# Gate and up from bare FP4 values in three of four scale groups, the PSUM bank rescaled three times per tile, and weight pieces spread from the second to last chunk on

## The reference, cut to what matters

```python
s_full = jnp.repeat(s, group_size, axis=1)
return vals * s_full
...
w_gu = _dequant_fp4(gate_up_packed, gate_up_scales, GROUP_SIZE)
w_down = _dequant_fp4(down_packed, down_scales, GROUP_SIZE)
gate_up = jnp.einsum('bsh,oh->bso', x, w_gu)
gate, up = (gate_up[..., :I], gate_up[..., I:])
h = jax.nn.silu(gate) * up
y = jnp.einsum('bsi,hi->bsh', h, w_down)
rms = jnp.sqrt(jnp.mean(y * y, axis=-1, keepdims=True) + EPS)
return y / rms
...
x = _layernorm(x + _L0_attn_ref(x, L0_attn_Wq, L0_attn_Wk, L0_attn_Wv, L0_attn_Wo, L0_attn_rms_w), axis=-1)
x = _layernorm(x + _L0_xattn_ref(x, fside_BxS2xS2_0, ctx_1024), axis=-1)
x = _layernorm(x + _L0_ffn_ref(x, L0_ffn_gate_up_packed, L0_ffn_gate_up_scales, L0_ffn_down_packed, L0_ffn_down_scales), axis=-1)
```

## Time and profile before

| | us |
|---|---|
| median of 3 runs (772.44 to 775.64) | 773.85 |
| profiled execution | 770.9 |
| its span | 769.1 |
| TensorE busy | 706.7 (92%) |
| VectorE busy | 495.7 (64%) |
| ScalarE busy | 379.9 (49%) |
| GpSimd busy | 195.7 (25%) |
| attention to the last piece | 0 to 345.8 |
| FFN | 345.8 to 769.1 |

### The profile page before, as it was taken

The page is one execution under the profiler, slowest core; times in us unless marked ns, Lnnn a source line. Parts: engine busy times, 40 slices in busy tenths (PEclk is TensorE's granted clock), DMA queues, the critical chain, the costliest instruction groups (busy, mean ns, idle before and its releaser), DMA issues.

```text
span 769.1 us, 11695 instructions
## 1 busy us (share of the span) xinstructions
PE 706.7 (92%) x4565; PEld 569.7 (74%) x4574; DVE 495.7 (64%) x956; ACT 379.9 (49%) x613; POOL 195.7 (25%) x229
## 2 busy tenths in 40 slices
PE   5899998999999899649999999999989999999993
PEld 4688787877777787536787867878767878778882
DVE  4658668784576855776856586858668666743334
ACT  5244463355634372384473655635473736552334
POOL 0544444343644366841021100102000211000000
PEclk9899999999999999769999999999999999999998
DMA  9500200100320040021002120000430001200031
GB/s 335 195 20 1 56 2 3 54 2 28 107 73 2 28 152 1 1 109 55 1 7 77 55 73 37 2 28 0 164 110 0 1 29 57 108 1 1 0 110 55
DMA packets 25408, 41.17 MB, mean 54 GB/s; under 512 B 5002, under 2 KB 7690, under 8 KB 25226
## 3 DMA queue, kind: packets, MB, share of 16 engines
q1 hardware_dynamic: 23194, 37.40, 14.1%
q10 hardware_dynamic: 2160, 3.02, 1.1%
HBM read 28.88 MB, written 11.53 MB: 53 GB/s over the span
## 4 chain that ended last, share of the span: by engine, by line
PE 66%; DVE 19%; ACT 8%; DMA 2%; issue 2%; POOL 1%; ACTq 0%; DVEq 0%; POOLq 0%
PE ps L1726 20%; PE ps L1742 13%; PE ps L1309 10%; DVE act_s L383 4%; PE ps L1393 3%; PE ps L1348 3%; PE ps L534 2%; PE ps L1703 2%; PE ps L543 2%; PE ps L1704 2%; DMA rms_col<-in_L_attn_rms_w_dram 2%; DVE masked L1228 2%; PE ps L1376 2%; PE ps L1369 1%; PE ps L1357 1%
## 5 line engine op out<-in xcount | busy, mean ns | idle before, releaser
L1726 PE MATMUL ps<-x2T_hi,weights 128*128 128x512 f32 x528 | 163.3, 390 | 0.0
L1726 PEld LDWEIGHTS ps<-x2T_hi,weights 128*128 128x128 f32 x528 | 99.2, 188 | 19.9
L1742 PE MATMUL ps<-weights,h_hi 128*128 128x512 f32 x352 | 110.3, 394 | 3.2 <-DVE h_lo L1588 3.2
L1726 PE MATMUL ps<-x2T_lo,weights 128*128 128x512 f32 x264 | 106.8, 405 | 0.3 <-DVE ps L1593 0.3
L1611 DVE TENSOR_TENSOR silu<-ps,silu 128x512 f32<-128x512 f32 x44 | 30.3, 689 | 99.3 <-PE ps L1726 99.1
L1309 PE MATMUL ps<-wqkv_lo,xT_hi 128*128 128x512 f32 x192 | 81.0, 422 | 9.0 <-DVE wqkv_lo L1177 5.0
L1742 PEld LDWEIGHTS ps<-weights,h_hi 128*128 128x128 f32 x352 | 65.4, 188 | 17.6 <-DVE h_lo L1588 3.9
L1309 PE MATMUL ps<-wqkv_hi,xT_lo 128*128 128x512 f32 x192 | 76.3, 397 | 0.0
L1309 PE MATMUL ps<-wqkv_hi,xT_hi 128*128 128x512 f32 x192 | 76.3, 397 | 0.0
L1105 POOL TENSOR_TENSOR rot<-qkv,tab 128x256 f32<-128x256 f32 x64 | 44.6, 731 | 114.6 <-ACT qkv L994 114.6
L1506 ACT ACTIVATE silu<-ps 128x512 f32<-128x512 f32 x44 | 26.3, 598 | 86.4 <-PE ps L1726 86.4
(11 more groups left out here) (190 smaller groups left out, 1535.2 us busy)
## 6 DMA issues: line engine op xcount, KB each, us to landing
w<-in_fside_BxS2xS_dram SPq DMA_DIRECT2D x4, 1024.0 KB, 7.7
x_dram<-xb SPq DMA_DIRECT2D x4, 1024.0 KB, 4.3
xc<-x_dram SPq DMA_DIRECT2D x4, 1024.0 KB, 5.5
x_in<-in_x_dram SPq DMA_DIRECT2D x15, 256.0 KB, 3.4
xb<-x_dram SPq DMA_DIRECT2D x3, 1024.0 KB, 5.5
out_dram<-xc SPq DMA_DIRECT2D x3, 1024.0 KB, 4.3
z<-in_x_dram SPq DMA_DIRECT2D x3, 768.0 KB, 4.6
x_dram<-z SPq DMA_DIRECT2D x3, 768.0 KB, 3.5
```

The lines of the kernel that those rows point to most:

```text
L1726: last = nc.tensor.matmul(dst[:, :], lhs, rhs, start=False, stop=(k == NK - 1 and n == 2), skip_group_check=True)
L1742: last = nc.tensor.matmul(ps[c][:, :], lhs, rhs, start=(it == 0 and n == 0), stop=(it == NI - 1 and n == 2))
```

## The change

Groups 0 to 2 of gate and up are now bare (`BARE = 3`). After group 0 the bank is multiplied by s0/s1, after group 1 by s1/s2, after group 2 by s2; then group 3 follows scaled. So a half has 2+2+2+3 matmuls. The ratios are made once, on VectorE behind chunk 1 (`column_ratios`). Each bare pair but the first waits for the rescale before it. Bare pieces need no diagonal and no low part; every second of them is now copied by VectorE. The pieces start in chunk 14 and are spread differently: 13 in chunks 14 and 15, 9 behind chunk 15, 13 in FFN batch 0. The norm of the last attention batch (z) moves behind them into batch 0. Expert and output steps have new places, and place 1.5 now exists on all engines.

```diff
-EXPERT_STEPS = {"w_maxima": 2, ..., "round_x": 10, "clip_x": 10, "scale_w": 11, ...
+EXPERT_STEPS = {"w_maxima": 0, ..., "round_x": 10.5, "clip_x": 10, "scale_w": 10.5, ...
-OUTPUT_STEPS = {"rms": 2, "residual": 3, "moments": 14, "root": 21, "output": 26}
+OUTPUT_STEPS = {"rms": 1.5, "residual": 3, "moments": 15, "root": 21, "output": 27}
-UNSCALED = 0
+BARE = 3
-FIRST_BESIDE = 27
-PIECES_AT = {(14, "end"): (0, 1, 2), (15, "masks"): (3, 4, 5), (15, "split"): (6, 7),
-             (15, "end"): tuple(range(8, FIRST_BESIDE))}
+FIRST_BESIDE = 22
+PIECES_AT = {(14, "masks"): (0,), (14, "split"): (1, 2), (14, "end"): (3, 4, 5), (15, "masks"): (6, 7, 8, 9), (15,
+    "split"): (10, 11, 12), (15, "end"): (13, 14, 15, 16, 17, 18, 19, 20, 21)}
-PIECE_STEPS = {0: 27, 1: 28, 2: 29, 3: 30, 4: 31, 5: 32, 11: 33, 20: 34}
+PIECE_SLOTS = (0, 1.5, 2, 2, 3, 3, 5, 5, 7, 11, 11, 20, 27)
+LATE_STEPS = {"z_moments": 1, "z_root": 1.5, "z_shift": 2, "z_x1": 4.5}
...
     def lo(self, dve, m):
+        elif self.copied_by[m] == "dve":
+            dve.wait_ge(full, at + 1)
+            self.nc.vector.tensor_scalar(self.parts(m)[0], bank[:, 0:self.count(m) * P], 1.0, None, ALU.mult)\
+                .then_inc(drained, 1)
...
+        def column_ratios():
+            nc.vector.tensor_scalar(ratios, scales, 0.0, TINY, ALU.is_equal, ALU.mult).then_inc(ratio_step, 1)
+            nc.vector.tensor_tensor(ratios, scales, ratios, ALU.add).then_inc(ratio_step, 1)
+            nc.vector.reciprocal(inverse[:, first], ratios[:, later]).then_inc(ratio_step, 1)
+            nc.vector.tensor_tensor(ratios[:, first], scales[:, first], inverse[:, first], ALU.mult)\
+                .then_inc(weights.gate_up_cols_set, 1)
...
         def inner_tile(b, it, beside):
             hidden_hi(b, it)
             beside(3 * it + 1)
-            if it + 1 < NI:
-                scale_up(b, it + 1)
+            for k in range(BARE):
+                if it + 1 < NI:
+                    scale_up(b, it + 1, k)
+                if k == 0:
+                    beside(3 * it + 1.5)
             beside(3 * it + 2)
...
         def inner_tile(b, it, beside):
             if it + 1 < NI:
-                scale_gate(b, it + 1)
+                scale_gate(b, it + 1, 0)
             hidden_lo(b, it)
+            beside(3 * it + 1.5)
+            for k in range(1, BARE):
+                if it + 1 < NI:
+                    scale_gate(b, it + 1, k)
             beside(3 * it + 2)
...
+        def bare(b, it, k, half):
+            dst, scaled, part = ((ps[4], gate_scaled, gate_part), (ps[5], up_scaled, up_part))[half]
...
+            if k > 0:
+                pe.wait_ge(scaled, (b * NI + it) * BARE + k)
+            elif it > 0:
+                pe.wait_ge(h_done if half else silu_done, b * NI + it)
+            [values] = weights.gate_up(k, half, it)
+            nc.tensor.matmul(dst[:, :], values, x2T_lo[:, k, :], start=(k == 0), stop=False, skip_group_check=True)
+            nc.tensor.matmul(dst[:, :], values, x2T_hi[:, k, :], start=False, stop=True, skip_group_check=True)\
+                .then_inc(part, 1)
...
-            for k in range(1, NK):
+            for k in range(BARE, NK):
...
-            def next_unscaled(c):
+            def next_bare(c):
+                if it + 1 < NI:
+                    if c > 0:
+                        bare(b, it + 1, c - 1, 1)
+                    if 0 < c < BARE:
+                        bare(b, it + 1, c, 0)
                 if c == 1:
-                    if it + 1 < NI:
-                        unscaled_up(b, it + 1)
                     beside(3 * it + 1.5)
```

More of the change, by code:

```diff
@@ L154, in weight_pieces @@
     gate_up(0)
-    for pair in range(1, PAIRS - 2):
+    down(0)
+    gate_up(1)
+    down(1)
+    for pair in range(2, PAIRS):
+        down(2 * pair - 2)
         gate_up(pair)
-        down(2 * pair - 2)
         down(2 * pair - 1)
-    for it in range(2 * PAIRS - 6, 2 * PAIRS - 4):
-        down(it)
-    gate_up(PAIRS - 2)
-    gate_up(PAIRS - 1)
-    for it in range(2 * PAIRS - 4, NI):
-        down(it)
-    return pieces, at
+    down(NI - 1)
+    return pieces, (DOWN_AT[-1] + 4) * KB
 PIECES, WEIGHTS_W = weight_pieces()
@@ L195, in expert_order @@
                     yield from ((b, use) for use in USES_OF.get(name, ()))
-            if b == 1 and at in PIECE_STEPS:
-                yield ("piece", PIECE_STEPS[at])
+            if b == 1:
+                yield from (("piece", FIRST_BESIDE + n) for n, slot in enumerate(PIECE_SLOTS) if slot == at)
         yield from ((b, use) for use in EXPERT_USES[-2:])
@@ L1083, in scalar_program @@
             chunk(n)
-        for m in PIECES_AT[CHUNKS - 1, "end"]:
-            weights.hi(act, m)
-            if m == NORMALISE_PIECE:
-                beside(steps, CHUNKS - 1, 3)
-            if m == LN_ROOT_PIECE:
-                ln_root_of(B - 1)
-            if X1_PIECE <= m < X1_PIECE + NC:
-                x1_of(B - 1, (m - X1_PIECE,))
+        beside(steps, CHUNKS - 1, 3)
+        beside_pieces(weights.hi, act, CHUNKS - 1, "end")
+        late["act"] = {"z_root": lambda: ln_root_of(B - 1), "z_x1": lambda: x1_of(B - 1, range(NC))}
     def pool_program(pool):
@@ L1439, in ffn_programs, with place @@
     ln_eps, ffn_eps = biases[:, 0:1], biases[:, 1:2]
[L1441 removed]
+    def place(expert_steps, output_steps, b, piece=None, late_steps={}):
         def run(at):
@@ L1451, in run @@
                         steps[name](of)
-            if b == 0 and piece and at in PIECE_STEPS:
-                piece(PIECE_STEPS[at])
+            if b == 0:
+                for n, slot in enumerate(PIECE_SLOTS):
+                    if piece and slot == at:
+                        piece(FIRST_BESIDE + n)
+                for name, slot in LATE_STEPS.items():
+                    if slot == at and name in late_steps:
+                        late_steps[name]()
         return run
@@ L1543, in scalar_program @@
             if b == 0:
-                act.wait_ge(weights.unscaled_cols_set, 1)
-            scale_up(b, 0)
+                act.wait_ge(weights.gate_up_cols_set, 1)
+            for k in range(BARE):
+                scale_up(b, 0, k)
             if b > 0:
                 squares(b - 1, range(NC // 2))
-            beside = place(steps, output_steps, b, lambda m: weights.hi(act, m))
+            beside = place(steps, output_steps, b, lambda m: weights.hi(act, m), late["act"])
             for it in range(NI):
@@ L1578, in pool_program @@
             beside = place(steps, {}, b, next_diagonals)
-            for at in range(3 * NI):
+            for at in (3 * it + place for it in range(NI) for place in PLACES):
                 beside(at)
@@ L1674, in vector_program @@
             if b == 0:
-                dve.wait_ge(weights.unscaled_cols_set, 1)
+                dve.wait_ge(weights.gate_up_cols_set, 1)
             split_x2T(b)
-            beside = place(steps, output_steps, b, lambda m: weights.lo(dve, m))
+            beside = place(steps, output_steps, b, lambda m: weights.lo(dve, m), late["dve"])
             for it in range(NI):
@@ L1804, in tensor_program @@
                 inner_tile(b, it, beside)
-        down(B - 1, NI - 1, lambda c: None)
+        for c in range(NC):
+            down(B - 1, NI - 1, c)
     return sync_program, scalar_program, pool_program, vector_program, tensor_program
```

267 lines of the change are left out of this document (131 added, 136 removed), and 6 rows, old and new, of the table EXPERT_STEPS.

## The result

The changed kernel takes 820.57 us (median of 4 runs, 819.59 to 821.58), the kernel before 773.37 (772.44 to 775.64) on the same chip: ratio 1.0594, 95% interval 1.055 to 1.0639. It is slower by 47 us, where 20 were forecast. The span of the profiled execution is 817.7 us, 48.6 more than before.

The account below looks back on a forecast made before the run. TensorE was taken to bound all four FFN batches, with VectorE having 28 us of slack in three. Pieces -10, starts +8, batches 0 to 2 +7, +8, +8, batch 3 -1 gave +20 us: median 794, range 766 to 811.

Parts of the forecast that it names:

- Bound before, matmuls removed: FFN: TensorE bounds all four batches; 30 matmuls per tile in place of 34, at 0.227 us each, save at most 40 us.
- Pieces, -10, and +2 at the first start: Fewer, cheaper pieces between chunk 15 and the x2 transposes save 10 us; batch 0's first-tile rescales, unhidden, add 2.
- Bare tile 7.2, batch 3 at -1: Batch 3, without expert work: a tile takes 7.2 us against 7.71; with table loads the batch changes by -1 us.
- the loads' 4.0: Batch 3: table loads and root come onto the rescale chains, +2.8 us for `rms` and +1.2 for `root`.
- Starts, +2 each: First tile of each of 4 batches: two more rescale links, less six gate matmuls, add 2 us each, 8 in all.
- Loaded batches, +8 each: Batches 1 and 2: VectorE's work, forced gaps and remaining waits make 100.8 us against 93.0, +8 us each.
- the other waits, 7.2: VectorE in batch 1: waits for expert products 3.5, column maxima 1.9 and the output's root 1.8 us stay.
- The upper end of +13: Batches 1 and 2: upper bound, following the load ahead of silu and the rounding of x on ScalarE tile by tile.
- A sign that failed: Expected in the profile: TensorE idle ahead of bare pairs, released by VectorE's rescale, 10 us or more per loaded batch.
- Batch 0, +7: Batch 0: VectorE's work, gaps, waits and four bare copies, plus ScalarE's z operations, add 7 us (-1 to +14).
- Clock, 809 us at 0.13: Rival, chance 0.13: TensorE's clock halves after some 3.2 us of waiting between batches, costing 5 us three times, 809 us.
- The moved expert steps: New places of expert steps: those in the attention chunks put at nothing, no term for those in the FFN.

Follow-up runs that it names:

- bare2: Changed kernel with two bare groups in place of three, the third pair and its rescales dropped: 778.3 us, ratio 1.004 to 1.010 to the kernel before.
- after_noroot: Changed kernel with the square roots in the feed-forward batches made Identity, so ScalarE loads no table inside them: 809.6 us, ratio 1.036 to 1.050.
- the two experiments that shorten it: Changed kernel with the two added up rescales on 1 column in place of 512, 813.1 us; and with feed-forward square roots as Identity, 809.6 us.
- gate_narrow: Changed kernel with the two added gate rescales of each tile on 1 column in place of 512: 810.5 us, ratio 1.039 to 1.053.
- old_tables: Changed kernel with the expert's and output's step tables as before the change (33 numbers differ): 842.6 us, ratio 1.088 to 1.093.

## Why the prediction was right and wrong

- **Bound before, matmuls removed:** right. TensorE's 0.227 us per matmul gives 7.26 for bare2's 32 matmuls, measured 7.25.
- **Pieces, -10, and +2 at the first start:** right, -7.8; the row from chunk 15 to the transposes is 8.4 us.
- **Bare tile 7.2, batch 3 at -1:** right, 7.19 and -0.2; the loads' 4.0 came as 2.8 by experiment. One gate rescale follows the other after 1.60 us (1.64 forecast).
- **Starts, +2 each:** +3.0, +2.7, +3.3. after_noroot gives 1.9 per start for loads that before had for nothing, and leaves +1.0, +1.0 and +1.4 for the links, which I had at 2. I priced the links and left the load ahead of the first silu at nothing, so two errors pull against each other in this row.
- **Loaded batches, +8 each:** this step failed. It took VectorE's sum as the value: busy 81.2 and waits 9.8+2.6+7.2 = 19.6. Busy is 82.8, near enough, and the gaps of the gate's chain are 11.4 against 12.4. The term that was mis-sized is the other waits, 7.2 "that lie inside expert steps and stay": VectorE's timeline has 13.0 of them. Of those that were counted 3.8 are left (2.5+1.3). The 9.2 that the sum had at nothing are the product's wait for the up matmuls (3.1) and for silu (0.6), h_hi (2.6), smoothing factors (1.3) and short links between small steps. Some 4.8 us of this kind stood in the batch before too (h_hi 1.9) and belonged in the list. That gives the +14.2 and +13.9. The upper end of +13 was near that for a reason that holds only in part: it was to be ScalarE's work, and the two experiments that shorten it give back 1.9 and 2.3 us of the 14, with some 0.6 of each being the clock's (1.00 in batch 1 in both). The sum has a flaw of its own, which gate_narrow shows: 10.4 us less of VectorE's work is worth 3.7. Busy time and forced gaps of one engine are a lower bound of a chain over three; its waits have to be followed.
- **A sign that failed:** TensorE was to wait 10 us or more per loaded batch for VectorE's rescale. It waits 6.9. The rest of its 16 us of idle time is split among silu (1.5), an expert step (1.7) and many short waits.
- **Batch 0, +7:** +19.5, the same error and 5 us on top. With the pieces it took little more than batch 1 before (94.6 against 93.0), and takes 7 us more now. That VectorE waits for ScalarE's half of a piece there is in the trace (6.5 us, the longest 4.85, at 447.42); which piece costs how much was not tried, and neither was the work on z.
- **Clock, 809 us at 0.13:** the wait was forecast at 3.2 us and came as 4.3, the clock fell, and it cost 1.5 us over the three starts in place of 15, since other waits lay beside it. The second fall, behind the first silu, was not forecast; it costs some 0.6 us per batch.
- **The moved expert steps** are nowhere in the sum, which starts from the stretch with the old places. They are worth 22 us against these (old_tables), so without them the miss would have been larger still.

## What to carry to other kernels

When an engine with a small share of idle time is relieved by splitting its work into groups with a handover between them, count the handovers before the work: four matmuls less per tile should have saved 9 us in each loaded batch, and the handovers, with their rescales and the table loads that they uncovered, made it 14 longer. Where every queue is in order and a chain crosses three of them, follow it tile by tile; one engine's work and forced gaps give the least, and costs that hide one another show only when they are taken out together. A view of waits by window also counts a wait that ends at its first instruction: look where the longest one lies. Try half of such a change: here two bare groups, with the new pieces and two steps moved, came out level, and the third took 42.5 us more.
